# A five-stage pipelined decoder kernel on one core: stage results written where the next stage reads them, small operations moved between VectorE, GpSimd and ScalarE, and new orders for four engines

## The chip, the core and the metric

The kernel runs on one core of a Trainium2 chip. The metric is the device time in microseconds (us), median of several runs of the same program. Engines are named as in the profile: PE is TensorE's matmul, PEld its weight load, DVE is VectorE, ACT is ScalarE, POOL is GpSimd, SP is SyncE, which issues the DMAs. A line name such as L662 is a line of the kernel before.

## What is computed

32 samples of 128 tokens by 128 features go through a decoder block: self-attention with 16 heads whose queries, keys and values are the input itself, a post-norm, cross-attention to a context inside a band of 64 tokens, a post-norm, and two layers of a local transformer (8 heads of 64, rotary position coding, l2-normalised queries and keys, a gated MLP with gelu), with a last post-norm. Cut to what matters here:

```python
x = _layernorm(x + _L0_attn_ref(x, weight))                 # stage "self"
x = _layernorm(x + _L0_xattn_ref(x, ctx, ctx, Wq, ..., bo)) # stage "cross"
# two layers, stages "local0" and "local1":
h = shift_token(x); q, k, v = split(h @ wqkv)
q = q / clip(norm(q), 1e-12) * qs;  k = k / clip(norm(k), 1e-12) * ksc
q, k = rotary_xpos(q, k)
x = x + softmax(masked(8 q k^T)) v @ wo
h = shift_token(x); h = (h - mean) / sqrt(var + 1e-05) * lg + lb
a, g = split(h @ w1 + b1);  x = x + (a * gelu(g)) @ w2 + b2
# after both layers:
x = _layernorm(x + local(x))
```

`_layernorm` is `(x - mean) / sqrt(var + 1e-05)`.

## The kernel before

**Pipeline.** One sample is one tile of 128 by 128. The program runs 37 iterations n = 0 to 36. In iteration n the stages work on different samples: self (letter S, and Z for its values) on sample n-1, cross (C) on n-2, local layer 0's attention (A is its head part, D its tail part) and the first half of its MLP (M) on n-3, the second half of that MLP (O) and layer 1's attention (B, E) on n-4, and layer 1's MLP (N, P) on n-5; `SKEW` holds these lags. Iterations 0 to 5 are written out (the fill), 6 to 31 are one body in a loop on every engine (26 passes), and 32 to 36 are written out again (the drain), with parts missing at both ends. Iteration 32 still has every part; 33 has no self stage, 34 no cross stage, 35 and 36 less still.

**What sets the order.** Each part is a Python generator per engine; a `yield` ends a step. `ORDER_TENSOR`, `ORDER_VECTOR`, `ORDER_SCALAR` and `ORDER_GPSIMD` are strings of letters: `weave` takes the next step of the part that each letter names. So these four strings alone fix the order in which an engine issues its work in an iteration. Every engine runs its own instructions strictly in that order and meets the others only at semaphores. Since an engine stops at the first wait that isn't met, all work that its string puts behind that wait stands too.

**The steps that the change touches.**

- Between stages the result is written to an `out` tile by DVE (`normalise`, L932; L1076 for local0), POOL copies it into the next stage's `x` (L1152, L1165, L1172), PE transposes that `x` (L621, L662), ACT copies the transpose to SBUF (`xT`, L823 and L824), and PE's projections follow (L665, L668, L672).
- The normalisations need 1/sqrt(variance + eps). DVE makes mean and variance (`bn_stats`, `bn_aggr`, L1052 or L928), POOL adds eps into a tile `ve` (L1119) and raises it to -0.5 (L1122, into `rs`), DVE applies it (L932, L1055). There are five of these per iteration.
- The l2 norms of local attention: ACT squares (L828), DVE sums (`ss`, L1016), POOL applies the floor 1e-24 (`sc`, L1188) and the power -0.5 (`rn`, L1191). There are four per iteration (keys and queries of two layers). POOL also adds the two rotary products (L1195 for keys, L1199 for queries), scales the keys (L1203) and, after the exponentials, multiplies `e` by the inverse sums (L1212).
- Self's scores are made twice: once in bf16 from `kb` and `qmb` for the row maximum (L518), then in f32 from `kT` and `qm` (L529) with the negated maximum added by a second product (L534). ACT's exponentials of the first pair of banks (L779) must be done before PE may fill the banks again with the second pair (the second L529, which waits for `exp_done`).
- ACT changes between gelu (L873) and exp (L779 or L848) twice per iteration. Each change needs an ACT_TABLE_LOAD, which the compiler puts directly ahead of the first activation of the other kind.

## Time and profile before

| | |
|---|---|
| time, median of 3 runs | 1459.94 us (1458.5 to 1462.15) |
| the profiled execution's own time | 1461.15 us |
| its span in the trace | 1459.3 us |
| steady pass of the loop (between two L572 of the trace, 1204.59 and 1246.59) | 42.00 us |
| iteration 32's L572 (the first after the loop) to the end | 170.8 us |
| TensorE clock over the span | 0.965 of full |

The page of the profile gives each engine's busy time as a share of the span, with the span in 40 slices beneath. The timeline gives instructions in order of time: start, duration, engine, line, operation, output and input tiles, shapes, and in brackets the idle time of that engine just before, with what ended it. A PE entry's duration runs past the start of the next one, because matmuls overlap at their ends; the distance between two starts is what a group takes of the engine.

### The profile page before, as it was taken

To read this page: it belongs to the slowest core of one execution; us is meant where nothing else is said; L and a number is where in the kernel's file an instruction comes from. 1 tells how busy PE (TensorE), PEld (TensorE's weight loads), DVE (VectorE), ACT (ScalarE), POOL (GpSimd) and SP (SyncE) were. 2 spreads that over 40 slices of the span, in tenths; PEclk is the share of its full clock that TensorE was granted. 3 is DMA by queue.
4 is the path that set the end of the run, shared out by engine and by line. 5 is a ranking of instruction groups with operands and counts; after the bars stand their busy time and mean duration, and the time that the engine had idled before them with its cause. 6 is when DMAs were issued, how large, how long until landed. Compare 5 with 4: busy or idle time off the path is not lost. (4 is left out here: it accounts for less than half of the span.)

```text
span 1459.3 us, 39524 instructions
## 1 busy us (share of the span) xinstructions
PE 1333.5 (91%) x12472; PEld 928.8 (64%) x12472; DVE 1026.3 (70%) x2900; ACT 938.5 (64%) x2563; POOL 885.3 (61%) x1291
## 2 busy tenths in 40 slices
PE   5889999999999999999999999999999999998864
PEld 3556666666666666666666666666666666666543
DVE  2467776777777777777777777777777777776431
ACT  1256765677776667777766677776666777765552
POOL 2046666666666666666667666666666666666542
PEclk8799999999999999999999999999999999998785
DMA  5000000000000000000000000000000000000000
GB/s 158 10 5 4 5 7 7 5 4 5 4 4 5 5 5 5 4 4 4 5 5 5 5 5 4 4 4 5 5 5 5 4 5 3 5 5 3 3 3 4
DMA packets 22220, 12.55 MB, mean 9 GB/s; under 512 B 5878, under 2 KB 21024, under 8 KB 22176
## 3 DMA queue, kind: packets, MB, share of 16 engines
q1 hardware_dynamic: 21600, 10.96, 2.6%
q10 hardware_dynamic: 576, 1.05, 0.2%
q8 instruction: 22, 0.36, 0.1%
q14 instruction: 22, 0.18, 0.0%
HBM read 9.91 MB, written 2.10 MB: 8 GB/s over the span
## 5 line engine op out<-in xcount | busy, mean ns | idle before, releaser
L1212 POOL TENSOR_TENSOR local_e<-local_e,local_rd 128x512 f32<-128x512 f32 x128 | 133.0, 1039 | 238.2 <-DVE local_rd L1033 238.2
L848 ACT ACTIVATE local_e<-local_ps,local_bias,local_rn 128x128 f32<-128x128 f32 x512 | 230.8, 482 | 7.3 <-DVE local_bias L1029 7.3
L1191 POOL TENSOR_TENSOR local_rn<-local_sc,half_neg 128x8 f32<-128x8 f32 x128 | 211.3, 1658 | 14.4
L586 PE MATMUL self_ps<-self_z,self_e 128*128 128x129 f32 x1024 | 155.8, 291 | 2.6 <-ACT self_e L779 1.4
L1024 DVE TENSOR_REDUCE local_m<-local_ps 128x4 f32<-128x512 f32 x128 | 87.8, 686 | 96.4 <-PE local_ps L509 96.4
L586 PEld LDWEIGHTS self_ps<-self_z,self_e 128*128 128x128 f32 x1024 | 130.7, 196 | 13.8 <-issue 2.7
L955 DVE SCALAR_TENSOR_TENSOR self_y<-self_ps,self_rd,self_y 128x128 f32<-128x128 f32 x448 | 133.3, 345 | 8.8 <-issue 0.6
L606 PE MATMUL local_ps<-wz,self_kT 128*128 128x512 f32 x256 | 134.1, 627 | 1.1 <-ACT local_v L832 0.6
L848 ACT ACTIVATION_READ_ACCUMULATOR local_e<-local_ps,local_bias,local_rn 128x1 f32 x512 | 117.4, 229 | 0.0
L828 ACT ACTIVATE local_sq<-local_ps 128x512 f32<-128x512 f32 x128 | 76.1, 595 | 61.4 <-PE local_ps L665 58.4
L665 PE MATMUL local_ps<-wqkv_s,local_xT 128*128 128x512 f32 x128 | 71.4, 639 | 26.6 <-ACT local_xT L824 26.6
L918 DVE TENSOR_REDUCE self_neg<-self_ps 128x4 bf16<-128x512 f32 x128 | 81.9, 681 | 16.6 <-DMA bo_r<-bo 10.0
L1007 DVE TENSOR_TENSOR local_cosp<-local_ps,cos_t 128x512 f32<-128x512 f32 x128 | 87.4, 683 | 6.5 <-ACT local_sq L828 6.2
L859 ACT ACTIVATE local_oT<-local_ps 128x512 f32<-128x512 f32 x64 | 40.1, 627 | 78.8 <-PE local_ps L709 78.8
L855 ACT ACTIVATE local_eT<-local_ps 128x512 f32<-128x512 f32 x128 | 70.9, 610 | 28.6 <-PE local_ps L703 28.5
L779 ACT ACTIVATE cross_e<-cross_ps 128x512 f32<-128x512 f32 x128 | 69.6, 601 | 27.4 <-PE cross_ps L499 27.4
L1011 DVE TENSOR_TENSOR local_sinp<-local_ps,sin_t 128x512 f32<-128x512 f32 x128 | 87.1, 681 | 0.0
L703 PE MATMUL local_ps<-con,local_e 128*128 128x128 f32 x512 | 76.2, 284 | 11.6 <-POOL local_e L1212 11.6
L1195 POOL TENSOR_TENSOR local_cosp<-local_cosp,local_sinp 128x512 f32<-128x512 f32 x64 | 81.1, 1267 | 5.7 <-DVE local_sinp L1011 5.7
L918 DVE TENSOR_REDUCE cross_neg<-cross_ps 128x4 bf16<-128x512 f32 x128 | 82.2, 683 | 3.3 <-PE cross_ps L499 3.0
L1016 DVE TENSOR_REDUCE local_ss<-local_sq 128x8 f32<-128x512 f32 x128 | 83.9, 676 | 0.0
L798 ACT ACTIVATE self_z<-local_ps 128x512 f32<-128x512 f32 x128 | 77.0, 603 | 9.5 <-PE local_ps L606 9.5
(172 smaller groups left out, 3392.6 us busy)
## 6 DMA issues: line engine op xcount, KB each, us to landing
self_xin<-x SPq DMA_DIRECT2D x32, 64.0 KB, 1.8
cross_cin<-ctx_in SPq DMA_DIRECT2D x32, 64.0 KB, 1.8
out<-local_out SPq DMA_DIRECT2D x32, 64.0 KB, 1.6
wqkv_s<-wqkv SPq DMA_DIRECT2D x2, 768.0 KB
wz<-w_heads ACTq DMA_DIRECT2D x4, 256.0 KB, 6.3
w_r<-w SPq DMA_DIRECT2D x2, 341.0 KB
con<-consts SPq DMA_DIRECT2D x1, 640.0 KB, 6.0
wo_s<-wo SPq DMA_DIRECT2D x2, 256.0 KB
```

Of the source, the lines that this page charges most:

```text
L586: last = nc.tensor.matmul(bank[:, 129 * j:129 * j + 129], s.e[:, h0 + j, :], s.z[:, h0 + j, :], start=True, stop=True)
L606: nc.tensor.matmul(LOC[l].b1 if g % 2 else LOC[l].b0, s.kT[:, :], wz[:, 512 * g:512 * g + 512], start=True, stop=True).then_inc(s.z_psum, 4)
L848: nc.scalar.activation(s.e[:, a, p, :], bank[:, 128 * p:128 * p + 128], ACT.Exp, bias=s.bias[:, a, p:p + 1], scale=s.rq[:, a, p:p + 1], ac ...
L918: nc.vector.tensor_reduce(s.neg[:, 32 * g:32 * g + GH], (s.odd if g % 2 else s.even).rearrange("p (j t) -> p j t", j=GH), AX.X, ALU.max, n ...
L955: nc.vector.scalar_tensor_tensor(out=s.y[:, h % 2, :], in0=bank[:, j, 0:128], scalar=s.rd[:, h:h + 1], in1=before, op0=ALU.mult, op1=ALU.a ...
L1007: nc.vector.tensor_tensor(s.cosp[:, a, :, :], heads, cos_t[l][:, a, :].unsqueeze(1).to_broadcast([128, LH, LD]), ALU.mult)\
L1011: nc.vector.tensor_tensor(s.sinp[:, a, :, :].rearrange("p h (u d) -> p h u d", u=2), halves[:, :, ::-1, :], sin_t[l][:, a, :].rearrange("p ...
L1016: nc.vector.tensor_reduce(s.ss[:, LH * a:LH * a + LH], s.sq[:, a, :, :], AX.X, ALU.add)\
L1024: nc.vector.tensor_reduce(s.m[:, a, :], bank.rearrange("p (c t) -> p c t", c=LH // 2), AX.X, ALU.max, negate=True)\
L1191: nc.gpsimd.tensor_tensor(s.rn[:, heads], s.sc[:, heads], half_neg[:, 0:LH], ALU.pow).then_inc(done, 8)
L1195: nc.gpsimd.tensor_tensor(s.cosp[:, 0, :, :], s.cosp[:, 0, :, :], s.sinp[:, 0, :, :], ALU.add).then_inc(s.k_roped, STEP)
L1212: nc.gpsimd.tensor_tensor(s.e[:, a, :, :], s.e[:, a, :, :], s.rd[:, a, :].unsqueeze(2).to_broadcast([128, LH // 2, 128]), ALU.mult)\
```

## The change

1. `normalise` writes self's result straight into cross's `x`, cross's result straight into local0's `x`, and L1076's sum straight into local1's `x`. The POOL copies into those tiles go, and so do the tiles `out` in between. PE's transposes now wait for DVE's signals (`cross_normed` and the like) instead of `x_copied`. Where the residual of the whole local block is needed later, POOL copies local0's `x` once into `keep`.
2. The addition of eps (`ve`) and the floor (`sc`) move from POOL to DVE, each right behind the instruction that makes its input, with a wait for it. POOL keeps the powers alone, now one step each.
3. Self's bf16 copies `kb` and `qmb` move from POOL to ACT.
4. Copying self's input into `self_x` stays on POOL. The table loads stay where they were, ahead of their first use.
5. All four order strings are new.

```diff
 ORDER_TENSOR = (
-    "OONAAONASPBPABPBCZSCBZSZZASACSBBDCSECSSCSDSDSDCSDEEMCCECME")
+    "ONOAAONABSPPBABPZSZBCSAAZCSDSCZSCBBSCSECSDDSSDCSDEEMCCECME")
...
-    "NANNSCBOBSSASAAAAABBBBBBAABDDEEPMMMSPSCC")
+    "NNSBASAAAABABBBBDDCEEMPMSCO")
...
                 nc.scalar.activation(s.kT[:, :], s.b0[:, 0:128], ACT.Copy).then_inc(s.xT_ready, STEP)
+                nc.scalar.activation(s.kb[:, :], s.b0[:, 0:128], ACT.Copy).then_inc(s.k_ready, STEP)
+                yield
+                act.wait_ge(s.q_wide, v + STEP)
+                nc.scalar.activation(s.qmb[:, :, :], s.qm[:, :, :], ACT.Copy).then_inc(s.low, STEP)
...
-                nc.vector.bn_aggr(s.mv[:, :], s.st[:, 0, :]).then_inc(s.moments, 8)
+                nc.vector.bn_aggr(s.mv[:, :], s.st[:, 0, :]).then_inc(s.moments, 4)
+                dve.wait_ge(s.moments, v + 12)
+                nc.vector.tensor_scalar(s.ve[:, :], s.mv[:, 1:2], EPS, None, ALU.add).then_inc(s.moments, 4)
...
                 if again(v):
-                    dve.wait_ge(LOC[0].x_copied, v)
-                normalise(s, v, s.out[:, :])
+                    dve.wait_ge(LOC[0].kept, v)
+                    dve.wait_ge(LOC[0].mid_done, v)
+                normalise(s, v, LOC[0].x[:, :])
...
                     nc.vector.tensor_reduce(s.ss[:, LH * a:LH * a + LH], s.sq[:, a, :, :], AX.X, ALU.add)\
-                        .then_inc(s.square_sum, 8)
+                        .then_inc(s.square_sum, 4)
+                    dve.wait_ge(s.square_sum, v + 8 * a + 4)
+                    nc.vector.tensor_scalar(s.sc[:, LH * a:LH * a + LH], s.ss[:, LH * a:LH * a + LH], 1e-24, None, ALU.max)\
+                        .then_inc(s.square_sum, 4)
...
-                    copy(s.x[:, 0, :], CROSS.out[:, :]).then_inc(s.x_copied, STEP)
+                        pool.wait_ge(LOC[1].base_bias, v)
+                    copy(s.keep[:, :], s.x[:, :]).then_inc(s.kept, STEP)
...
-                    nc.gpsimd.tensor_scalar(s.sc[:, heads], s.ss[:, heads], 1e-24, 1.0, ALU.max, ALU.mult).then_inc(done, 8)
-                    yield
-                    pool.wait_ge(done, v + 8)
-                    nc.gpsimd.tensor_tensor(s.rn[:, heads], s.sc[:, heads], half_neg[:, 0:LH], ALU.pow).then_inc(done, 8)
+                    nc.gpsimd.tensor_tensor(s.rn[:, heads], s.sc[:, heads], half_neg[:, 0:LH], ALU.pow).then_inc(done, STEP)
```

What the new strings do to the engines' order is shown at three places. The first is TensorE in the middle of the loop body, from the first pair of self's f32 scores (L529 with L534) to the second pair, which waits for the two exponentials of the first. Before:

```order
L529 MATMUL self_ps<-self_qm,self_kT 128x512 x2
L534 MATMUL self_ps<-self_negT,hot_b 128x128 x8
L678 MATMUL local_ps<-con,local_cosp 128x128 x4
L653 REGISTER_ALU
L685 MATMUL local_ps<-con,local_cosp 128x128 x4
L696 MATMUL local_ps<-local_kT,local_qT 128x128 x8
L509 MATMUL local_ps<-mask_n,ident_b 64x512 x4
L552 REGISTER_ALU
L518 MATMUL cross_ps<-cross_kb,cross_qmb 128x128 x8
L499 MATMUL cross_ps<-mask_w,ident_b 64x4x64 x4
L529 MATMUL self_ps<-self_qm,self_kT 128x512 x2
```

The same stretch of TensorE in the changed kernel:

```order
L529 MATMUL self_ps<-self_qm,self_kT 128x512 x2
L534 MATMUL self_ps<-self_negT,hot_b 128x128 x8
L518 MATMUL cross_ps<-cross_kb,cross_qmb 128x128 x8
L499 MATMUL cross_ps<-mask_w,ident_b 64x4x64 x4
L606 MATMUL local_ps<-wz,self_kT 128x512
L529 MATMUL self_ps<-self_qm,self_kT 128x512 x2
```

Between the two pairs the transposes L678 and L685, the local scores L696 and their mask L509 have gone elsewhere, and one value product L606 has come in.

The second place is ScalarE at the same point of the changed kernel's loop body, with the semaphore that an instruction waits for in brackets. Lines are those of the changed kernel (its L852 was L848, its L802 was L798).

```order
L815 ACTIVATE cross_kT<-cross_ps,bk_c 128x128
L779 ACT_TABLE_LOAD [waits self_scores_t_psum]
L779 ACTIVATE self_e<-self_ps 128x512
L779 ACTIVATE self_e<-self_ps 128x512 [waits self_scores_t_psum]
L852 ACTIVATE local_e,local_den<-local_ps,local_bias,local_rn 128x128 [waits local0_bias_ready]
```

As before, the table load carries the wait for the scores; the two exponentials now follow each other directly, where before a copy of local1's `qT` stood between them.

The third place is GpSimd, where it handles the rotary sums and the norms of the two layers. Before, from the start of layer 1's part:

```order
L1195 TENSOR_TENSOR local_cosp<-local_cosp,local_sinp 128x512
L1188 TENSOR_SCALAR local_sc<-local_ss 128x8
L1191 TENSOR_TENSOR local_rn<-local_sc,half_neg 128x8
L1199 TENSOR_TENSOR local_cosp<-local_cosp,local_sinp 128x512
L1203 TENSOR_TENSOR local_cosp<-local_cosp,local_rn 128x512
L1188 TENSOR_SCALAR local_sc<-local_ss 128x8 x2
L1191 TENSOR_TENSOR local_rn<-local_sc,half_neg 128x8 x2
```

And in the changed kernel (L1183, L1187, L1179 and L1191 are there what L1195, L1199, L1191 and L1203 were):

```order
L1183 TENSOR_TENSOR local_cosp<-local_cosp,local_sinp 128x512
L1179 TENSOR_TENSOR local_rn<-local_sc,half_neg 128x8 x2
L1187 TENSOR_TENSOR local_cosp<-local_cosp,local_sinp 128x512
L1191 TENSOR_TENSOR local_cosp<-local_cosp,local_rn 128x512
L1179 TENSOR_TENSOR local_rn<-local_sc,half_neg 128x8
```

The floors have left GpSimd, and the first of the two powers in a row is now that of layer 0's queries; before, it stood behind all of layer 1's rotary work.

## Rows read from the trace of the kernel before

**Rows 1.** The page, part 1: busy time, share of the span, instructions.

```profile
PE 1333.5 (91%) x12472; PEld 928.8 (64%) x12472; DVE 1026.3 (70%) x2900; ACT 938.5 (64%) x2563; POOL 885.3 (61%) x1291
```

**Rows 2.** One pass: length, busy time of PE, PEld, DVE, ACT, POOL (count), clock.

```profile
1204.59:1246.59 42.00, 40.14 (x390) 28.18 (x389) 31.90 (x91) 29.13 (x80) 27.57 (x41) 1.00 0.02 5
```

**Rows 3.** Timeline of PE at the start of a pass.

```profile
737.95 0.33 PE L727 MATMUL cross_ps<-local_mid,con 128*128 128x64 f32 x2
738.90 0.30 PE L662 MATMUL local_ps<-con,local_x 128*128 128x128 f32 x1 [0.62 <-issue]
740.01 1.10 PE L665 MATMUL local_ps<-wqkv_s,local_xT 128*128 128x512 f32 x2 [0.81 <-ACT local_xT L824]
```

**Rows 4.** Timeline of DVE and POOL at the same place.

```profile
737.88 0.37 DVE L932 TENSOR_SCALAR cross_out<-cross_r,cross_mv,cross_rs 128x128 f32<-128x128 f32 x1 [0.69 <-POOL cross_rs L1122]
...
738.50 0.30 POOL L1096 TENSOR_SCALAR local_x<-cross_out 128x128 f32<-128x128 f32 x1 [0.35 <-DVE cross_out L932]
```

**Rows 5.** Timeline of PE, its other two idle gaps of a pass.

```profile
727.01 1.09 PE L709 MATMUL local_ps<-local_eT,local_v 128*64 128x128 f32 x16 [0.20 <-ACT local_eT L855]
...
735.64 1.16 PE L715 MATMUL local_ps<-wo_s,local_oT 128*128 128x128 f32 x8 [0.23 <-ACT local_oT L859]
```

**Rows 6.** Instruction groups of POOL and DVE: busy, mean ns | idle before.

```profile
L1191 POOL TENSOR_TENSOR local_rn<-local_sc,half_neg 128x8 f32<-128x8 f32 x128 | 211.3, 1658 | 14.4
L1199 POOL TENSOR_TENSOR local_cosp<-local_cosp,local_sinp 128x512 f32<-128x512 f32 x64 | 81.3, 1271 | 0.0
L1203 POOL TENSOR_TENSOR local_cosp<-local_cosp,local_rn 128x512 f32<-128x512 f32 x64 | 66.6, 1041 | 0.0
L1188 POOL TENSOR_SCALAR local_sc<-local_ss 128x8 f32<-128x8 f32 x128 | 32.0, 250 | 10.8 <-DVE local_ss L1016 0.2
L1096 POOL TENSOR_SCALAR self_qmb<-self_qm 128x512 bf16<-128x512 f32 x32 | 19.8, 617 | 0.3 <-POOL self_qm L1136 0.3
...
L1119 POOL TENSOR_SCALAR local_ve<-local_mv 128x1 f32<-128x1 f32 x96 | 18.3, 190 | 74.0 <-DVE local_mv L1052 63.7 <-DVE local_mv L928 7.7
```

**Rows 7.** Timeline of PE and ACT in the fill, no table load there.

```profile
18.47 0.39 PE L534 MATMUL self_ps<-self_negT,hot_b 32*128 32x128 bf16 x8
...
18.95 1.08 ACT L779 ACTIVATE self_e<-self_ps 128x512 f32<-128x512 f32 x2 [0.52 <-PE self_ps L534]
...
20.09 2.08 PE L529 MATMUL self_ps<-self_qm,self_kT 32*128 32x512 f32 x4 [1.23 <-ACT self_e L779]
```

**Rows 8.** Timeline of ACT in the drain: a table load behind a wait.

```profile
1390.62 1.28 ACT L848 ACT_TABLE_LOAD   x1 [1.87 <-DVE local_bias L1029]
```

**Rows 9.** Timeline of PE: what L606, L518 and L499 take.

```profile
708.66 1.02 PE L606 MATMUL local_ps<-wz,self_kT 128*128 128x512 f32 x2
709.62 0.40 PE L518 MATMUL self_ps<-self_kb,self_qmb 32*128 32x128 bf16 x8
...
717.18 0.40 PE L518 MATMUL cross_ps<-cross_kb,cross_qmb 32*128 32x128 bf16 x8
...
717.79 1.13 PE L529 MATMUL self_ps<-self_qm,self_kT 32*128 32x512 f32 x4
```

**Rows 10.** Timeline of POOL and DVE while POOL multiplies.

```profile
721.99 1.04 POOL L1212 TENSOR_TENSOR local_e<-local_e,local_rd 128x512 f32<-128x512 f32 x1 [3.12 <-DVE local_rd L1033]
...
722.66 0.39 DVE L1029 TENSOR_TENSOR local_bias<-local_m,local_rn 128x4 f32<-128x4 f32 x1
```

**Rows 11.** Timeline of POOL and DVE during a short POOL addition.

```profile
232.00 0.45 POOL L1223 TENSOR_TENSOR local_midb<-local_mid,local_base 128x128 f32<-128x128 f32 x1
232.13 0.41 DVE L932 TENSOR_SCALAR cross_out<-cross_r,cross_mv,cross_rs 128x128 f32<-128x128 f32 x1 [0.69 <-POOL cross_rs L1122]
```

**Rows 12.** Timeline of DVE at the end of a pass, first and last.

```profile
731.03 0.29 DVE L1039 TENSOR_TENSOR local_mid<-local_ps,local_x 128x128 f32<-128x128 f32 x1 [0.24 <-PE local_ps L715]
...
734.62 0.34 DVE L1057 TENSOR_SCALAR local_hn<-self_ps,local_mv,local_rs 128x64 f32<-128x64 f32 x1
```

**Rows 13.** Timeline of PE in iteration 34: the wait for weights.

```profile
1395.30 0.99 PE L703 MATMUL local_ps<-con,local_e 128*128 128x128 f32 x4 [4.38 <-POOL local_e L1212]
```

More of the change, by code:

```diff
@@ L1038, in attention_tail @@
                     dve.wait_ge(s.mid_bias, v)
-                nc.vector.tensor_tensor(s.mid[:, :], s.b1[:, 0:128], s.x[:, 0, :], ALU.add).then_inc(s.mid_done, STEP)
+                nc.vector.tensor_tensor(s.mid[:, :], s.b1[:, 0:128], s.x[:, :], ALU.add).then_inc(s.mid_done, STEP)
                 yield
@@ L1074, in mlp_tail @@
                     if again(v):
-                        dve.wait_ge(LOC[1].x_copied, v)
-                    nc.vector.tensor_tensor(s.out[:, 0, :], s.m0[:, 0:128], s.midb[:, :], ALU.add).then_inc(s.resid, STEP)
+                        dve.wait_ge(LOC[1].mid_done, v)
+                    nc.vector.tensor_tensor(LOC[1].x[:, :], s.m0[:, 0:128], s.midb[:, :], ALU.add).then_inc(s.resid, STEP)
                     yield
@@ L1083, in mlp_tail @@
                         dve.wait_ge(stored, v)
-                    normalise(s, v, s.out[:, 0, :])
+                    normalise(s, v, s.out[:, :])
                 yield
@@ L1114, in prepare_local, with inverse_root @@
                 pool.wait_ge(prep_v, PREP_V_LOCAL)
-            def inverse_root(s, v, moments_done, mv, out, done):
+            def inverse_root(s, v, moments_done, ve, out, done):
                 pool.wait_ge(moments_done, v + STEP)
-                nc.gpsimd.tensor_scalar(s.ve[:, :], mv[:, 1:2], EPS, 1.0, ALU.add, ALU.mult).then_inc(done, 8)
-                yield
-                pool.wait_ge(done, v + 8)
-                nc.gpsimd.tensor_tensor(out, s.ve[:, :], half_neg[:, 0:1], ALU.pow).then_inc(done, 8)
+                nc.gpsimd.tensor_tensor(out, ve[:, :], half_neg[:, 0:1], ALU.pow).then_inc(done, STEP)
             def self_stage(v):
@@ L1133, in self_stage @@
                 pool.wait_ge(s.xT_ready, v + STEP)
-                copy(s.kb[:, :], s.kT[:, :]).then_inc(s.k_ready, STEP)
-                yield
                 nc.gpsimd.tensor_tensor(s.qm[:, :, :], s.kT[:, :].unsqueeze(1).to_broadcast([128, GH, 128]), head_rows, ALU.mult)\
                     .then_inc(s.q_wide, STEP)
-                yield
-                pool.wait_ge(s.q_wide, v + STEP)
-                copy(s.qmb[:, :, :], s.qm[:, :, :]).then_inc(s.low, STEP)
                 if not again(v):
@@ L1151, in cross_stage @@
                     pool.wait_ge(s.resid, v)
-                copy(s.x[:, :], SELF.out[:, :]).then_inc(s.x_copied, STEP)
-                nc.gpsimd.tensor_tensor(s.xb[:, :], SELF.out[:, :], bo_r[:, :], ALU.add).then_inc(s.x_bias, STEP)
+                nc.gpsimd.tensor_tensor(s.xb[:, :], s.x[:, :], bo_r[:, :], ALU.add).then_inc(s.x_bias, STEP)
                 yield
-                yield from inverse_root(s, v, s.moments, s.mv, s.rs[:, :], s.rstd)
+                inverse_root(s, v, s.moments, s.ve, s.rs[:, :], s.rstd)
                 yield
```

53 lines of the change are left out of this document (20 added, 33 removed).

## The prediction

> **What bounds the kernel now.** I read the page first. TensorE is busy for 91% of the span, no other engine for more than 70% [rows 1]. I then cut one pass of the loop out of the windows view: 42.00 us, of which TensorE is busy 40.14 at full clock, while VectorE has 31.90, ScalarE 29.13 and GpSimd 27.57 [rows 2]. So TensorE's own work is the bound, and only 1.86 us per pass can be won by placing things better. TensorE's timeline shows where these lie, and there are four places. It waits 0.62 us before the transpose L662 and 0.81 us before L665 [rows 3], 0.20 before L709 and 0.23 before L715 [rows 5]. The first is a chain over three engines: VectorE writes cross's result (737.88 to 738.25), GpSimd copies it (738.50 to 738.80), and L662 starts at 738.90 [rows 3, 4]. The second is ScalarE's copy of the transpose, which the change leaves as it is.
>
> What matters is therefore not how busy VectorE or GpSimd get, but whether TensorE, which runs strictly in order, finds each input ready. I walked through the changed order with durations from the trace, one pass long.
>
> **Gains in a pass.** The GpSimd copy of 0.30 us and its two hand-overs go, and L662 can start when VectorE has written. GpSimd's eps addition (0.19 us [rows 6]) leaves the same chain and a VectorE one comes in, about even. VectorE had written by 738.25 and TensorE was free at 738.28 (738.90 less 0.62), so the whole 0.62 goes. L665 still follows L662 and a ScalarE copy directly: the 0.81 stays. The 0.20 before L709 goes if TensorE arrives later there than before, which the losses below see to. GpSimd loses about 3.9 us of its 27.6 per pass and ScalarE gains about 0.9 (0.62 for `qmb` [rows 6] and about 0.3 for `kb`); neither is on TensorE's path, since GpSimd mostly waits and ScalarE has 13 us idle.
>
> **Loss 1: the exponentials of self.** The changed TensorE order puts only L518, L499 and one L606 between the first pair of self's scores and the second. The second pair may not start before ScalarE has done two exponentials. In the fill, where no table load is needed, the L529 starts 1.23 us after L534 ended (two exponentials of 1.08 us together and the hand-overs) [rows 7]. In the loop the load of exp's table comes first. It is placed behind the wait for the scores: in the drain the same kind of load stood idle for 1.87 us until the value that its activation needed was there, and took 1.28 us [rows 8]. So the second pair can start 1.23 + 1.28 = 2.51 us after L534's end. In between TensorE has L518 and L499, 0.61 us from start to start (717.18 to 717.79), and L606 with 0.96 (708.66 to 709.62) [rows 9], and L518 begins 0.07 before L534 ends (0.39 of duration, 0.32 from start to start): 1.50 us of cover. That leaves TensorE idle for 1.01 us. Before, 3 us of work stood there and it cost nothing. The idle could be smaller only if the load came before the wait, and larger if L852's predecessor were late; I take 1.01, with 0.9 and 1.2 as bounds. Everything between L534 and this L529 that comes late is absorbed here.
>
> **Loss 2: VectorE's small operations behind GpSimd.** Four floors and five eps additions per pass come to VectorE. The trace has none there. The nearest rows are GpSimd's own 0.25 and 0.19 us [rows 6], and I take 0.25 for each with the wait for its predecessor. But some may cost more. A VectorE addition of 128x4 numbers that met a GpSimd multiplication ran 0.39 us and ended at 723.05, GpSimd's at 723.03 [rows 10]. A VectorE tensor_scalar of the kind that is now added, normally 0.37 [rows 4], ran 0.41 when GpSimd's addition lasted until 232.45, and ended 0.09 later [rows 11]. This is the pattern of an operation that is held until GpSimd lets go. The Trainium skill says so in SBUF — State Buffer, "SBUF: two separate sides": a VectorE operation in a two-port mode or with two SBUF inputs and a GpSimd operation exclude each other for a whole instruction. By that rule, the trace agrees, each added operation could wait out a full instruction of GpSimd.
>
> In the new orders layer 0's key floor falls due about 0.2 us after GpSimd begins `qm`, which takes as long as the key scaling (1.04 us [rows 6]); it would then hold VectorE for about 0.8 us. The floor for the queries comes late by the next rotary sum (1.27 us [rows 6]), by 0.1 to 0.3. Behind them on VectorE stand the gate product, for which L750 waits, and self's row maxima, for which L556 waits. With the distance that VectorE has there I get 0.3 at the first and 0.2 at the second: 0.5 us per pass. Bounds: 0 if the floors pass freely, and 1.3 if each is held for a whole rotary sum.
>
> **Loss 3: the end of the pass.** From layer 0's `mid` to its last normalised half VectorE takes 3.93 us (731.03 to 734.96) [rows 12]. Three eps additions join (0.75), and so does local1's normalisation (0.35, mostly overlapped: 0.25), while `self_r` may lose 0.2 that it spent beside a GpSimd addition. That is 0.8 later for L731 and, behind it, L715. L715 had waited for ScalarE until 735.64, 0.68 after VectorE was done [rows 5, 12], and 0.1 of this is L731 itself. So 0.6 is hidden and 0.2 is left, the old gap of 0.23 included. Bounds 0 and 0.8.
>
> **The pass:** -0.62 - 0.20 + 1.01 + 0.5 + 0.2 = +0.9 us, so 42.9. It applies to the 26 loop passes and to iterations 4, 5 and 32, which look the same: 29 x 0.9 = 26 us.
>
> **Fill and drain.** Here TensorE does wait for chains. The power for layer 0's queries used to stand behind layer 1's rotary work on GpSimd: a floor, a power, a rotary sum, a key scaling and two more floors, 0.25 + 1.66 + 1.27 + 1.04 + 0.5 = 4.7 us [rows 6]. It now stands ahead of these. Layer 0's exponentials need it, and TensorE then waited 4.38 us for their weights in iteration 34 [rows 13]. I put the gain at 4 us there, 4 in iteration 33 and 2 for 35 and 36 (shorter copies, an earlier L662): 10 us, bounds 4 and 14. In the first iterations shorter hand-overs and the earlier exponentials give 2 us, bounds -2 and 4.
>
> **Sum:** +26 - 10 - 2 = +14 us. The span is 1459.3, the profiled execution 1461.15 and the median of the runs 1459.94, so I add to the median: 1474 us, 1% slower.
>
> **Rivals.**
>
> - The small operations pass. The VectorE additions are not held, and the end of the pass has room: -0.62 - 0.20 + 1.01 = +0.2 per pass, 6 us in all, less 12 at the ends: 1454 us. For it: a 128x8 operation is short and most of GpSimd's time is one power, beside which I saw no hold. Chance 0.25. It spans 1448 to 1466.
> - Faster, one mechanism: the exponentials of self don't stop TensorE. If the table load ran ahead of the scores, 1.23 us would be needed against 1.50 of cover. With all of 0.62, 0.20 and 0.23 gone the pass is 40.95, 29 x 1.05 = 30 less, and 12 at the ends: 1418; with 0.5 of VectorE's delays, 1432. The point from which it decides is a load that begins before L534 ends. Against it: [rows 8]. Chance 0.12.
> - VectorE turns into the bound of stretches. By the skill's rule, if all four floors and the eps additions are held for whole GpSimd instructions (1.04 to 1.66 us) and the delays add up, the pass grows by 2 us: +58 - 12 = 1506 us. Against it: GpSimd's power did not hold VectorE, and VectorE has 10 us idle [rows 2]. Chance 0.12.
> - The change does nothing to the time: passes gain in one place what they lose in another, and the ends too, 1460 us. Chance 0.08.
> - The forecast, 1465 to 1486 us: 0.43.
>
> **How the numbers follow.** About 0.3% (4.4 us) is what a measurement of this kernel can tell from no change. Faster: the second rival (0.12) and 0.14 of the first, 0.26. Same: 0.09 of the first, 0.08 of the fourth and 0.03 of the forecast's low edge, 0.20. Slower: the rest, 0.54. The range 1446 to 1492 leaves out the faster rival but for 0.01 and the third but for 0.03; that is 0.2.
>
> **What the changed profile would show.** The idle before L662 gone, 0.81 before L665 unchanged; about 1 us idle before the second self L529, ended by ScalarE's `self_e`; the `sc` instructions of VectorE, some of 0.9 us instead of 0.15, ending with GpSimd's instruction; short gaps at the second L750 and at L556; L731 waiting for `local_hn`. A pass of 42.9 us, and a distance from iteration 32's L572 to the end of about 161 us. I am wrong if the L529 starts without a gap, if `sc` is always short, or if TensorE's clock falls below full in the loop.

## The result, and the profile after

The changed kernel takes 1483.26 us (median of 4 runs, 1481.8 to 1485.39), beside 1460.2 for the kernel before on the same chip. The ratio is 1.016, 95% interval 1.0139 to 1.0178: 1.6% slower, 9 us above the forecast of 1474 and inside its range. The profiled execution has a span of 1480.0 us; it is the fastest of the four and the one with the highest mean clock (0.963, the others 0.956 to 0.958). Line numbers are those of the changed kernel from here on, and those of its own file for each experiment (some lie a few lines off).

The page, part 1, the answer to [rows 1]:

```profile
PE 1331.0 (90%) x12472; PEld 927.5 (63%) x12472; DVE 1099.8 (74%) x3188; ACT 968.9 (65%) x2627; POOL 762.6 (52%) x843
```

TensorE does the same work in a longer span. VectorE has 288 instructions and 73.5 us more, GpSimd 448 instructions and 123 us less.

Two passes from the windows view (length, busy time of PE, PEld, DVE, ACT, POOL, granted clock), the answer to [rows 2]:

```profile
1183.70:1226.49 42.79, 39.90 (x391) 27.98 (x390) 34.05 (x101) 30.07 (x82) 23.74 (x26) 1.00 0.02 5
1226.49:1270.51 44.02, 41.32 (x391) 29.43 (x390) 34.17 (x101) 30.07 (x82) 23.73 (x26) 0.96 0.02 4
```

There are two kinds of pass. Most take 42.77 us, 0.77 more than before. Five of the 25 between iterations 7 and 32 take about 44.03, and only in these is the granted clock below 1.

The timeline of PE in the first of these passes, with every idle gap that the view marks (those over 0.15 us) and what stands before the long one; the answer to [rows 3, 5, 9]:

```profile
1188.07 0.93 PE L750 MATMUL cross_ps<-w_s,local_gate 114*128 114x128 f32 x6 [0.20 <-DVE local_gate L1079]
...
1198.09 0.22 PE L534 MATMUL self_ps<-self_negT,hot_b 32*128 32x128 bf16 x2
1198.11 0.22 PE L518 MATMUL cross_ps<-cross_kb,cross_qmb 32*128 32x128 bf16 x2
1198.26 0.30 PE L499 MATMUL cross_ps<-mask_w,ident_b 64*64 64x256 bf16 x4
1198.49 1.13 PE L606 MATMUL local_ps<-wz,self_kT 128*128 128x512 f32 x2
1200.81 1.13 PE L529 MATMUL self_ps<-self_qm,self_kT 32*128 32x512 f32 x4 [1.20 <-ACT self_e L779]
...
1203.64 0.91 PE L586 MATMUL self_ps<-self_z,self_e 128*128 128x129 f32 x6 [0.20 <-ACT self_e L779]
...
1219.97 0.30 PE L731 MATMUL self_ps<-con,local_hn 128*128 128x128 f32 x1 [0.34 <-DVE local_hn L1070]
...
1222.73 0.27 PE L662 MATMUL local_ps<-con,local_x 128*128 128x128 f32 x1
1223.81 1.10 PE L665 MATMUL local_ps<-wqkv_s,local_xT 128*128 128x512 f32 x2 [0.81 <-ACT local_xT L828]
```

L662 no longer waits, L709 and L715 neither, and the 0.81 before L665 is unchanged. New are 1.20 us before the second L529, 0.20 before L586, 0.20 before L750 and 0.34 before L731. L556 waits 0.14 here, just under what the view marks.

ScalarE at the long gap, the answer to [rows 8]:

```profile
1198.38 1.28 ACT L779 ACT_TABLE_LOAD   x1 [1.92 <-PE self_ps L534]
1199.68 1.09 ACT L779 ACTIVATE self_e<-self_ps 128x512 f32<-128x512 f32 x2
```

ScalarE stood idle for 1.92 us ahead of the load of exp's table, which began when L534's scores were there.

VectorE's first two floors of the pass, and GpSimd beside them:

```profile
1185.06 0.98 DVE L1027 TENSOR_SCALAR local_sc<-local_ss 128x8 f32<-128x8 f32 x1
1189.90 0.23 DVE L1027 TENSOR_SCALAR local_sc<-local_ss 128x8 f32<-128x8 f32 x1
```

```profile
1184.98 1.04 POOL L1144 TENSOR_TENSOR self_qm<-self_kT,con 128x512 f32<-128x512 f32 x1 [2.59 <-ACT self_kT L785]
1188.84 1.27 POOL L1187 TENSOR_TENSOR local_cosp<-local_cosp,local_sinp 128x512 f32<-128x512 f32 x1
```

Each floor began while GpSimd was at work and ended 0.02 us after GpSimd's instruction (1186.04 after 1186.02; 1190.13 after 1190.11). The other two floors of the pass take 0.17.

**Where the 20.7 us between the two profiled spans lie.** From the starts of L572: up to iteration 7 the changed kernel is 0.9 us ahead. The 25 passes from there to iteration 32 take 1075.48 us against 1049.94: 25 x 0.77 = 19.2, and 5 x 1.26 = 6.3 for the passes with a lower clock. From iteration 32 to the end it is 166.9 against 170.8, 4 us less. In that start each kernel has one pass at a granted clock of 0.96, the changed one from iteration 4 to 5 (43.48 us), the kernel before from 6 to 7 (44.16).

### The profile page after: what moved, and what is told of

The parts are those of the page before. It is cut to its first block and busy times, and to the rows that moved or that the text cites. A ratio compares the mean times of both kernels' runs of the same rounds, so it can differ in the third digit from the quotient of the medians.

```text
span 1480.0 us, 39442 instructions
## 1 busy us (share of the span) xinstructions
PE 1331.0 (90%) x12472; PEld 927.5 (63%) x12472; DVE 1099.8 (74%) x3188; ACT 968.9 (65%) x2627; POOL 762.6 (52%) x843
## 5 line engine op out<-in xcount | busy, mean ns | idle before, releaser
L1179 POOL TENSOR_TENSOR local_rn<-local_sc,half_neg 128x8 f32<-128x8 f32 x128 | 210.1, 1648 | 208.3 <-DVE local_sc L1027 125.3
L852 ACT ACTIVATE local_e<-local_ps,local_bias,local_rn 128x128 f32<-128x128 f32 x512 | 236.7, 495 | 40.5 <-DVE local_bias L1040 40.5
L586 PE MATMUL self_ps<-self_z,self_e 128*128 128x129 f32 x1024 | 157.4, 297 | 8.4 <-ACT self_e L779 7.2
L586 PEld LDWEIGHTS self_ps<-self_z,self_e 128*128 128x128 f32 x1024 | 135.7, 200 | 23.7 <-issue 13.5
L606 PE MATMUL local_ps<-wz,self_kT 128*128 128x512 f32 x256 | 144.7, 648 | 1.8 <-ACT self_kT L785 1.0
L802 ACT ACTIVATE self_z<-local_ps 128x512 f32<-128x512 f32 x128 | 76.9, 601 | 91.6 <-PE local_ps L606 91.6
L852 ACT ACTIVATION_READ_ACCUMULATOR local_e<-local_ps,local_bias,local_rn 128x1 f32 x512 | 124.1, 242 | 0.0
L529 PE MATMUL self_ps<-self_qm,self_kT 32*128 32x512 f32 x256 | 74.3, 657 | 36.2 <-ACT self_e L779 34.9
L1132 POOL TENSOR_TENSOR local_rs<-local_ve,half_neg 128x1 f32<-128x1 f32 x96 | 53.3, 556 | 82.3 <-DVE local_ve L1065 67.1
L665 PE MATMUL local_ps<-wqkv_s,local_xT 128*128 128x512 f32 x128 | 68.9, 620 | 26.6 <-ACT local_xT L828 26.6
L1183 POOL TENSOR_TENSOR local_cosp<-local_cosp,local_sinp 128x512 f32<-128x512 f32 x64 | 81.5, 1274 | 10.4 <-DVE local_sinp L1019 10.4
```

Source lines behind the costliest of these rows:

```text
L586: last = nc.tensor.matmul(bank[:, 129 * j:129 * j + 129], s.e[:, h0 + j, :], s.z[:, h0 + j, :], start=True, stop=True)
L606: nc.tensor.matmul(LOC[l].b1 if g % 2 else LOC[l].b0, s.kT[:, :], wz[:, 512 * g:512 * g + 512], start=True, stop=True).then_inc(s.z_psum, 4)
L852: nc.scalar.activation(s.e[:, a, p, :], bank[:, 128 * p:128 * p + 128], ACT.Exp, bias=s.bias[:, a, p:p + 1], scale=s.rq[:, a, p:p + 1], ac ...
L1179: nc.gpsimd.tensor_tensor(s.rn[:, heads], s.sc[:, heads], half_neg[:, 0:LH], ALU.pow).then_inc(done, STEP)
L1183: nc.gpsimd.tensor_tensor(s.cosp[:, 0, :, :], s.cosp[:, 0, :, :], s.sinp[:, 0, :, :], ALU.add).then_inc(s.k_roped, STEP)
```

## The experiments

Times are medians of 4 runs (e2 of 5). The ratio is to the kernel before, run beside each on the same chip, where it took 1462 to 1464 us (beside the changed kernel 1460.2, the first row), so ratios compare better than times from row to row. "Pass" is the distance of two L572 in the loop, from one profiled execution each.

| kernel | orders | on VectorE | exp table load | pass, us | time, us | ratio (95%) |
|---|---|---|---|---|---|---|
| before | old | - | | 42.00 | 1460.2 | 1 |
| e5 direct writes only | old | - | | 41.29 | 1438.47 | 0.984 (0.982-0.986) |
| e14 and kb, qmb on ScalarE | old | - | | 41.50 | 1445.39 | 0.988 (0.985-0.990) |
| e9 | old | floors | | 41.78 | 1450.72 | 0.991 (0.989-0.994) |
| e7 all code | old | floors, eps | | 42.71 | 1479.05 | 1.012 (1.010-1.013) |
| after | new | floors, eps | behind the wait | 42.77 | 1483.26 | 1.016 (1.014-1.018) |
| e2 | new | eps | behind the wait | 42.22 | 1473.97 | 1.009 (1.007-1.011) |
| e1 | new | floors, eps | early | 41.49 | 1436.56 | 0.982 (0.979-0.984) |
| e15 | new | 3 floors, eps | early | 42.00 | 1451.13 | 0.992 (0.988-0.995) |
| e6 | new | eps | early | 40.93 | 1420.65 | 0.972 (0.969-0.975) |
| e6b | new | - | early | 40.90 | 1420.02 | 0.972 (0.969-0.974) |
| e11 = e6, L662 earlier | new* | eps | early | 40.65 | 1412.17 | 0.965 (0.963-0.967) |
| e13 = after, more cover | new* | floors, eps | behind the wait | 43.32 | 1486.67 | 1.016 (1.014-1.018) |
| e8 = after, one load more | new | floors, eps | behind, and slower | 45.0 | 1569.95 | 1.074 (1.071-1.076) |

### The exponentials' gap: e1, e8, e13

The early load is one line more, behind the copy of cross's keys on ScalarE:

```diff
                 nc.scalar.activation(s.kT[:, :], s.b0[:, 0:128], ACT.Identity, bias=bk_c[:, :]).then_inc(s.k_ready, 8)
+                nc.scalar.activation(warm[:, :], SELF.z[:, 0, 128:129], ACT.Exp)
```

> The changed kernel with one more ScalarE instruction: an exponential of one column (128x1, its result is used by nobody) right behind the copy of cross's keys (L815), so that the exp table is loaded there and not behind the wait for self's scores (in the changed kernel the load at L779 stood idle for 1.92 us and then took 1.28). Theory A, the table load makes the gap: without it the second pair of self's scores needs 1.23 us after L534's end against 1.50 us of cover, so the 1.20 us of idle before the second L529 goes, and with it the 0.20 before L586; the five passes with a granted clock of 0.96 go too if the gap is what brings the clock down. Pass 41.4 us, 29 x 1.4 = 41 and 6 for the clock: 1483 - 47 = 1436 us. Rival B, the gap only hides another bound (VectorE's chain of the pass is late anyway): the idle time turns up at L556, L586 or L731, the pass falls by 0.4 at most, 1471 us.

It came out as theory A has it: 1436.56 us, pass 41.49. ScalarE in its timeline, and PE's second L529, which has no bracket and so no idle before it:

```profile
1074.38 1.28 ACT L816 ACT_TABLE_LOAD   x1
1075.67 0.20 ACT L816 ACTIVATE warm<-self_z 128x1 f32<-128x1 f32 x1
1076.30 1.08 ACT L779 ACTIVATE self_e<-self_ps 128x512 f32<-128x512 f32 x2 [0.42 <-PE self_ps L534]
```

```profile
1077.45 1.13 PE L529 MATMUL self_ps<-self_qm,self_kT 32*128 32x512 f32 x4
```

The load now lies in time in which ScalarE had nothing to do. The pass lost 1.28 us, just the load's length, and none of the 25 passes is below full clock in the profiled execution. The 0.2 before L586 stayed, which the expectation had wrong. The next run turns the screw the other way.

```diff
                 act.wait_ge(s.scores_t_psum, v + 4 * k + 4)
+                if s is SELF and k == 0 and again(v):
+                    nc.scalar.activation(warm2[:, :], SELF.z[:, 0, 128:129], ACT.Gelu)
```

> The opposite of the early load: the changed kernel with a second table load behind the wait for self's scores. ScalarE loads exp early (small exponential behind L815), then, behind the wait for L534's scores, runs a gelu of one column (its result is used by nobody), which needs a load of 1.28 us, and the exponentials need exp loaded again, 1.28. TensorE's idle before the second L529 becomes 1.20 + 1.28 + about 0.2. Theory A, this idle is what brings TensorE's clock down for some microseconds: more than 5 of the 25 passes show a granted clock below 1, and the gap's own cost is 1.5 us per pass: 1483 + 29 x 1.5 = 1527 us, and 1.25 for each further pass with a lower clock, up to 1550. Rival B, the lower clock has nothing to do with the idle: 5 passes again or fewer, 1527 us at most. Rival C, part of the longer gap is absorbed by work that waited later in the pass (L586, L731): 1515.

It took 1570 us, more than theory A's upper end. The gap did not grow as I had thought: ScalarE ran the gelu load ahead of the wait, but three loads of 1.28 then stood in a row and exp's ended at 681.73, so TensorE was idle for 2.32 us. PE at that gap, and two passes in the windows view:

```profile
682.88 1.23 PE L530 MATMUL self_ps<-self_qm,self_kT 32*128 32x512 f32 x4 [2.32 <-ACT self_e L782]
```

```profile
664.68:709.67 44.99, 41.17 (x392) 29.20 (x391) 34.07 (x101) 33.25 (x86) 23.72 (x26) 0.96 0.02 4
709.67:756.32 46.65, 42.86 (x392) 30.23 (x391) 34.16 (x101) 33.40 (x86) 23.73 (x26) 0.93 0.01 4
```

All 25 passes lie below full clock: 16 at 0.96 and 9 at 0.93. So the idle brings the clock down, and a longer one does it more often and for longer. Why a gap of 1.20 us does it in some passes and not in others stays open. In the changed kernel the place can be seen in small windows behind the gap, which ended at 1243.58:

```profile
1242.00:1244.00 2.00, 0.80 (x3) 0.30 (x4) 1.48 (x4) 1.99 (x6) 0.00 (x0) 1.00 0.00 0
1244.00:1246.00 2.00, 2.00 (x30) 1.34 (x27) 0.71 (x2) 2.00 (x8) 0.00 (x0) 0.90 0.00 0
1246.00:1248.00 2.00, 2.00 (x12) 1.80 (x10) 1.45 (x4) 2.00 (x7) 0.41 (x1) 0.50 0.00 0
1248.00:1250.00 2.00, 2.00 (x20) 1.88 (x20) 1.23 (x5) 1.65 (x9) 2.00 (x2) 0.74 0.00 0
```

TensorE has been back at work for 2 us when its clock falls to 0.50 (1.2 GHz instead of 2.4), and it is busy all through the last three windows. Their clocks of 0.90, 0.50 and 0.74 over 2 us each make 3.4 us at half clock in all.

The third run of this group leaves the load and adds cover, one L606 more between the two pairs (order strings of TensorE and ScalarE, one Z each moved):

```diff
-    "ONOAAONABSPPBABPZSZBCSAAZCSDSCZSCBBSCSECSDDSSDCSDEEMCCECME")
+    "ONOAAONABSPPBABPZSZBCSAACSDSCZZSCBBSCSECSDDSSDCSDEEMCCECME")
...
-    "OAANBSAPBASZZBBCAAZSCSSDZDSSBBDCDECEDDCEEDCCEEEM")
+    "OAANBSAPBASZZBBCAASCSSDZZDSSBBDCDECEDDCEEDCCEEEM")
```

> The changed kernel with the table load left where it is, behind the wait for self's scores, but with one more value product L606 (0.95 us) between the two pairs: the third Z of the TensorE order moves behind the L518/L499 group, beside the fourth, and on ScalarE its copy L802 moves behind the two exponentials. Theory A (the prediction's account, 2.51 us needed against the work in between): cover rises by 0.95, the idle before the second L529 falls from 1.20 to 0.25, the pass from 42.77 to 41.85, and no pass falls below full clock: 1483 - 29 x 0.95 - 6 = 1449 us. Rival B, the place that L606 leaves was itself cover (for cross's xT, or self_neg): idle of up to 0.9 turns up there, and the time stays above 1465.

Rival B: 1486.67 us, pass 43.32. PE in its pass:

```profile
1073.12 0.22 PE L556 MATMUL self_ps<-ident_b,self_neg 128*128 128x128 bf16 x1 [1.01 <-DVE self_neg L922]
...
1078.64 1.13 PE L529 MATMUL self_ps<-self_qm,self_kT 32*128 32x512 f32 x4 [0.42 <-ACT self_e L779]
```

The gap at L529 shrank, and the place that L606 left opened by 1.01 us: that product had covered VectorE's row maxima. In this pass no work is to spare as cover. The same run says something on the clock: with idle of 1.01 and 0.42 us in two places all 25 passes are at full clock. That is no safe limit: in the kernel before, the pass from iteration 6 to 7 is at 0.96, and its clock falls at 234.9, behind two gaps of 0.89 and 0.81 us:

```profile
233.20 0.30 PE L662 MATMUL local_ps<-con,local_x 128*128 128x128 f32 x1 [0.89 <-issue]
234.30 1.42 PE L665 MATMUL local_ps<-wqkv_s,local_xT 128*128 128x512 f32 x2 [0.81 <-ACT local_xT L824]
```

### The small operations on VectorE: e2, e6, e6b, e15

Floors back on GpSimd (e2: alone; e6: with the early load):

```diff
-                        .then_inc(s.square_sum, 4)
-                    dve.wait_ge(s.square_sum, v + 8 * a + 4)
-                    nc.vector.tensor_scalar(s.sc[:, LH * a:LH * a + LH], s.ss[:, LH * a:LH * a + LH], 1e-24, None, ALU.max)\
-                        .then_inc(s.square_sum, 4)
+                        .then_inc(s.square_sum, 8)
...
+                    nc.gpsimd.tensor_scalar(s.sc[:, heads], s.ss[:, heads], 1e-24, 1.0, ALU.max, ALU.mult).then_inc(done, 8)
+                    pool.wait_ge(done, v + 8)
```

> The changed kernel with the four floors per pass (sc) back on GpSimd, each directly ahead of its power, and all else as it is. Theory A, VectorE's floors are held while GpSimd works: the first floor of a pass took 0.98 us on VectorE and ended 0.02 us after GpSimd's qm, the third and fourth about 0.17. Without them VectorE is 1.4 us freer per pass, the 0.20 before L750 and the 0.15 that shows before L556 in some passes go: pass 42.5, 29 x 0.25 = 7 us less, 1476. Rival B, what is lost in a pass is the exponentials' gap alone, and GpSimd's extra 0.25 us in front of each power cancels it: 1483 +- 3.

> The changed kernel with both edits that helped alone: the small exponential behind L815, so that the exp table is loaded early (pass 41.49, 1436.6 us), and the four floors back on GpSimd (pass 42.22). Theory A, the two losses are separate places and add up: 0.55 us less per pass than with the early load alone, pass 40.94, 1436.6 - 28 x 0.55 = 1421 us, no pass below full clock. Rival B, with the gap gone VectorE and GpSimd are what TensorE waits for next: idle time turns up elsewhere and the pass stays above 41.3, 1432 us or more.

Both went with theory A, and e2's pass fell by more than its expectation has: 0.55 us. In e2 L750 starts 0.36 us earlier in the pass and L556 0.55, while the 1.20 before L529 is untouched; 4 of its 25 passes are at a clock of 0.96, and the profiled execution, 1466.7 us, is the fastest of the five, so its pass and its median don't belong to the same execution. On top of the early load the gain is again 0.56, so the two losses add up. e6 is the first kernel here that beats both e1 and e5: 1420.65 us.

In e6b the eps additions go back in the same manner, behind each `bn_aggr` and ahead of each power.

> The kernel with early load and floors back on GpSimd, and the five eps additions (ve) back on GpSimd too: what is left of the change is the direct writes, kb and qmb on ScalarE, and the new orders. Theory A (Loss 3 of the prediction), the eps additions make VectorE's chain at the end of the pass late: the 0.34 us before L731 goes, 40.6 us per pass, 9 us less than with the early load and the floors alone, 1412. Rival B, L731 waits because the new TensorE order asks for local_hn earlier and not because of eps: the gap stays within 0.1, and the time within 3 us.

The time is rival B's, within 1 us: the five eps additions on VectorE cost 0.03 us per pass here. Its reason is not, since the 0.34 before L731 does go, as theory A has it. Counted from L727 ahead of them, L731 starts 3.99 us later in e6 and 3.51 in e6b, but L739 behind L715 5.02 and 5.00: without the eps additions L715 waits 0.19 for ScalarE instead. They make L731 late, and the wait behind it hides that.

In e15 only the floor with `(l, a) == (0, 0)`, layer 0's keys, goes back:

```diff
+                        .then_inc(s.square_sum, 8 if (l, a) == (0, 0) else 4)
+                    if (l, a) != (0, 0):
```

> The kernel with the early load (41.49 a pass, 1436.6 us), with one of the four floors back on GpSimd: that of layer 0's keys, which took 0.98 us on VectorE while GpSimd ran self's qm. The other three, 0.17 to 0.23 us each, stay on VectorE. With all four back the pass was 40.93. Theory A, the loss is this one meeting: at least 0.36 of the 0.56 us comes back (the shift of L750), pass 41.0 to 41.15, 1425 us. Rival B, the loss is the time that four instructions with their waits take on VectorE, whichever: a quarter comes back, pass 41.35, 1433 us. Rival C, another small instruction is now held in its place: pass 41.5.

This is rival C and worse than it: 15 us slower than e1, from one floor that went from VectorE to GpSimd. The timelines of DVE and POOL show why:

```profile
1038.19 1.12 DVE L1029 TENSOR_SCALAR local_sc<-local_ss 128x8 f32<-128x8 f32 x1
```

```profile
1038.02 1.27 POOL L1193 TENSOR_TENSOR local_cosp<-local_cosp,local_sinp 128x512 f32<-128x512 f32 x1
```

```profile
1041.15 0.40 PE L518 MATMUL self_ps<-self_kb,self_qmb 32*128 32x128 bf16 x8 [0.54 <-DVE self_neg L923]
```

VectorE reached the second floor 0.17 us after GpSimd had begun a rotary sum and was held until it ended (1039.31, GpSimd 1039.29). Self's row maxima stood behind it, and L518 and L556 waited 0.54 and 0.43 us. In e1 the same floor came 1.07 us after that sum's start and took 0.22. Both engines moved: counted from L572, the floor came 0.36 us earlier (5.84 instead of 6.20), and the sum began 0.54 later (5.68 instead of 5.14), because the first floor now stood on GpSimd ahead of its power. So the cost of a floor is not its length but where in a GpSimd instruction it falls. SBUF — State Buffer, "SBUF: two separate sides", in the Trainium skill says of the pair of ports that VectorE and GpSimd share, for VectorE operations in a two-port mode or with two SBUF inputs: whoever comes first has it for its whole instruction. These rows agree.

### The same code in the old orders: e5, e14, e9, e7

e5 is the changed kernel's direct writes with everything else as before. e7 is the changed kernel with the old strings, cut where a step is gone:

```diff
 ORDER_GPSIMD = (
-    "NNSBASAAAABABBBBDDCEEMPMSCO")
+    "NNSCOBSAAAAABBBBABDDEEMMPSC")
```

e9 is e7 with the eps additions back on GpSimd, and e14 is e9 with the floors back too.

> The kernel before with part 1 of the change alone: stage results written straight into the next stage's input, GpSimd's copies gone, keep copied where kept stood; floors, eps, kb and qmb on GpSimd and all four order strings as before. Theory A, the 0.62 us before L662 was pure gain and stays won: pass 42.00 - 0.62 = 41.4, 29 x 0.62 = 18, 2 us more in the drain: 1440 us. Rival B, the time won turns up as a longer wait at L709 (0.20 before) and L715 (0.23), which are set by chains that don't start at L662: pass 41.8, 1454 us.

Theory A: 1438.47 us, pass 41.29. The idle before L662 is gone, which starts 0.10 us after VectorE's `local_x` ended (1096.55):

```profile
1096.65 0.30 PE L662 MATMUL local_ps<-con,local_x 128*128 128x128 f32 x1
1097.76 1.10 PE L665 MATMUL local_ps<-wqkv_s,local_xT 128*128 128x512 f32 x2 [0.81 <-ACT local_xT L824]
```

The first part of the change alone is worth 24 us (1462.05 beside it).

> Old orders, direct writes, floors and eps on GpSimd, and of the moved operations only kb and qmb on ScalarE (in the old orders the pass was 41.29 with direct writes alone, 41.78 with the floors on VectorE and kb, qmb on ScalarE). Theory A, the 0.49 us between these two is the floors': pass 41.3, 1438 us. Rival B, it is qmb's 0.62 on ScalarE ahead of the squares and value copies: pass 41.8, 1451 us.

In between: `kb` and `qmb` on ScalarE cost 0.21 us per pass, where I had costed them at nothing. `kb` stands ahead of `sq`, the gelu and `xT` on ScalarE; `sq` starts about 0.15 later in the pass than in e5, `xT` (L828) ends about 0.15 later, at 1191.51, and L665, which needs it, starts at 1191.65, later by as much. In e5 L665 followed L672 with no wait.

> All code of the changed kernel (direct writes, floors and eps on VectorE, kb and qmb on ScalarE) with the four order strings of the kernel before, cut by the steps that are gone and with one step more for qmb on ScalarE. In this TensorE order 3 us of work stand between the two pairs of self's scores, so the exponentials cost nothing. Theory A, the new TensorE order is what made the change slow: the pass is -0.62 for the copies, and +0.3 to +0.5 for the small operations on VectorE, 41.8, 1453 us, with no idle before the second L529 and no pass below full clock. Rival B, the small operations on VectorE are what made it slow: pass 42.6 or more, 1477 us.

Rival B, 1479.05 us: the new TensorE order is not what makes the moved operations dear. VectorE, GpSimd and PE in this kernel's pass:

```profile
1071.10 0.15 DVE L934 TENSOR_SCALAR local_ve<-local_mv 128x1 f32<-128x1 f32 x1
1071.23 0.90 DVE L1040 TENSOR_TENSOR local_bias<-local_m,local_rn 128x4 f32<-128x4 f32 x1
```

```profile
1071.07 1.04 POOL L1200 TENSOR_TENSOR local_e<-local_e,local_rd 128x512 f32<-128x512 f32 x1 [0.85 <-DVE local_rd L1044]
```

```profile
1072.96 0.94 PE L586 MATMUL self_ps<-self_z,self_e 128*128 128x129 f32 x6 [0.82 <-DVE self_y L961]
```

An old instruction, `local_bias` of 128x4 numbers, is held until GpSimd ends, because an eps addition ahead of it made it 0.2 us late. The eps addition itself was not held: it began 0.03 us after the same product of GpSimd and took its usual 0.15.

> The kernel with all code of the change but the old orders (pass 42.71, 1479 us), with the five eps additions back on GpSimd. There an eps addition of 0.15 us on VectorE stood ahead of layer 0's second local_bias (L1040, 128x4): with its wait it moved that instruction from 1070.98 to 1071.23, past the start of GpSimd's product L1200 at 1071.07, and it took 0.90 us instead of 0.16 and ended with GpSimd's; self_y behind it was late and TensorE idle for 0.82 before L586. Theory A, this meeting is the main loss of that kernel: without the eps addition L1040 is through before GpSimd starts, the 0.82 goes, pass 41.6 to 41.9, 1450 us. Rival B, the floors on VectorE or qmb on ScalarE make self_y late: L1040 is short or not, and the pass stays above 42.4, 1470 us or more.

Theory A, 1450.72 us. `local_bias` starts before GpSimd's product and slips through:

```profile
1052.90 0.16 DVE L1038 TENSOR_TENSOR local_bias<-local_m,local_rn 128x4 f32<-128x4 f32 x1
```

```profile
1053.04 1.04 POOL L1198 TENSOR_TENSOR local_e<-local_e,local_rd 128x512 f32<-128x512 f32 x1 [0.85 <-DVE local_rd L1042]
```

It had 0.14 us to spare. In the old orders the eps additions cost 0.93 us per pass and the floors 0.28; in the new ones 0.03 and 0.56. The same instructions, other meetings. (The two pairs were not taken in the same order: in the old orders the eps additions came on top of the floors, in the new ones the floors on top of the eps additions.)

### A further step: e11

```diff
-    "ONOAAONABSPPBABPZSZBCSAAZCSDSCZSCBBSCSECSDDSSDCSDEEMCCECME")
+    "ONAOAONABSPPBABPZSZBCSAAZCSDSCZSCBBSCSECSDDSSDCSDEEMCCECME")
```

> The kernel with early load and floors on GpSimd (40.93 a pass, 1420.65 us), with the start of the TensorE order changed so that L662 of layer 0 stands ahead of the second group of MLP products (L744) and not behind it. L665 then has 0.75 us of work between it and L662, and waits only for ScalarE, which is at gelu (L877) until 0.2 us after L662's usual start and then copies for 0.58. Theory A: of the 0.81 before L665 about 0.5 goes, 0.2 comes back before L662, which now waits for VectorE's local_x: pass 40.65, 1413 us. Rival B, the second half of the MLP products is late by what L662 waits, and with it the gate product L750: pass 40.9, within 3 us of 1420. Rival C, worse, since L662 waits for the whole chain of cross's normalisation: 1430.

Theory A in the time: 1412.17 us, pass 40.65, 3.5% faster than the kernel before. The 0.81 before L665 is 0.24; half of what that frees is given back elsewhere in the pass, about 0.14 in waits too short for the view to mark and 0.14 in TensorE's busy time.

## Why the prediction was right, and where it wasn't

Between the profiled spans the change cost 20.7 us where 14 were forecast. The pass was nearly right, 0.77 instead of 0.9, which is 3 us less over 25 passes. The clock, which had no term, added 6. From iteration 32 on 4 us were won where 9 were forecast (10, less the 0.9 of iteration 32's pass). Up to iteration 7 the changed kernel was 0.9 us ahead where it should have been 0.7 behind; the first iterations were not taken apart. That the total came out so near is in part luck, for the terms of the pass are off by more than their sum. The runs give them as a chain from the kernel before to the changed one, one edit at a time except in the third row, which has two:

| edit | pass, us | difference | the prediction's term |
|---|---|---|---|
| before to e5: direct writes | 42.00 to 41.29 | -0.71 | -0.62 |
| e5 to e14: kb, qmb on ScalarE | to 41.50 | +0.21 | 0 |
| e14 to e6b: new orders, load early | to 40.90 | -0.60 | -0.20 |
| e6b to e6: eps on VectorE | to 40.93 | +0.03 | +0.2 (Loss 3, 0.23 of old gap included) |
| e6 to e1: floors on VectorE | to 41.49 | +0.56 | +0.5 (Loss 2) |
| e1 to after: load behind the wait | to 42.77 | +1.28 | +1.01 (Loss 1) |
| sum | | +0.77 | +0.9 |

The third row holds what the prediction had at nothing: the new order saves TensorE work. Where L518 follows L534 directly, the two groups run in turns and take 0.34 us together (1197.92 to 1198.26 in the changed kernel). In the old orders they stood apart, here in e14, with 0.32 from L534 to the next start and 0.33 from L518:

```profile
1202.91 0.39 PE L534 MATMUL self_ps<-self_negT,hot_b 32*128 32x128 bf16 x8
1203.23 0.66 PE L678 MATMUL local_ps<-con,local_cosp 128*128 128x128 f32 x4
...
1205.68 0.40 PE L518 MATMUL cross_ps<-cross_kb,cross_qmb 32*128 32x128 bf16 x8
1206.01 0.30 PE L499 MATMUL cross_ps<-mask_w,ident_b 64*64 64x256 bf16 x4
```

That is 0.31 us at each of two places in a pass, about 0.6, against the 0.20 that the prediction expected from L709. TensorE's busy time in a pass falls by less, from 40.12 us in e14 to 39.72 in e6b. No run changes this alone.

- **The gap before L662** went as forecast, and 0.09 more with shorter waits earlier in the pass.
- **The exponentials' gap** was the right mechanism with the right need: L534's last product ended at 1198.31, L529 started at 1200.81, 2.50 us where 2.51 was worked out [rows 7, 8]. Mis-sized was the cover, 1.50 us. L518 alternated with L534 instead of following it, so only 0.18 of L518 and L499 lay behind L534's end, where 0.54 was taken. L606 covers up to its own end, 1.12, where 0.96 was taken, the distance to a next start. Together 1.30, and the idle was 1.20.
- **VectorE held by GpSimd** was right in place (layer 0's key floor beside `qm`, the query floor by a rotary sum) and in size (0.36 at L750 and 0.19 at L556, where 0.3 and 0.2 stood). What I took from it was too simple: it is a cost of phase, and e15 shows that it can rise when a floor leaves VectorE. It is also not a cost of every small operation. The eps additions (128x1) take 0.153 to 0.157 us in all 160 cases each of the changed kernel and of e7, also beside GpSimd's product. So the first rival, that the small operations pass, was right for these five and wrong for the floors. The third, that all are held, did not come true: in the changed kernel one of four floors per pass lost more than 0.1 us.
- **The end of the pass** had the right mechanism and too large a size. The eps additions make L731 wait 0.34, and what ScalarE would have made L715 wait hides it: e6b against e6 leaves 0.03 of the forecast 0.2.
- **kb and qmb on ScalarE** were costed at nothing because ScalarE has 13 us idle per pass. That step was wrong: idle on average did not hide `kb` at the place where TensorE needs the `xT` that stands behind it, and it cost 0.21 (e14).
- **TensorE's clock** was the sign that I named for being wrong. It falls in 5 of 25 passes and costs 6.3 us. The prediction had no term for it, though it forecast the idle that brings it about; by its own sign it was wrong here.
- **The drain** gained 4 us, not 10. The wait of 4.38 us for the weights in iteration 34 [rows 13] did shrink:

```profile
1419.64 1.11 PE L703 MATMUL local_ps<-con,local_e 128*128 128x128 f32 x4 [1.07 <-POOL local_e L1200]
```

From L672 to L672 that iteration is 3 us shorter (36.3 instead of 39.3). But iteration 33, counted by the same L672, won 0.9 and not 4, since no such wait stood in it, and behind the last L672 nothing was won (38.7 us to the end in both). That step carried a wait of one iteration over to its neighbour without a row for it. The gain belongs to the new orders: from iteration 32 to the end the kernels with old orders take 170 to 172.6 us, those with new ones 164.3 to 166.9 (e8, with its long gaps, 168.6). That it is GpSimd's place for the layer 0 power, and no other letter, was not tried by itself.
- **Rival 2**, that the exponentials don't stop TensorE, named its condition: a load that begins before L534 ends. e1 makes it true and takes 1436.6, where the rival gave 1432 with VectorE's delays; e6 takes these away and takes 1420.7, where it gave 1418.

## What to carry to other kernels

An engine's table load that stands behind a wait belongs to the latency of the wait: where a compiler puts it at its first use, a small activation of the same table ahead of the wait moves it into idle time. Which side of the wait a load stands on is read from the trace, since e8's gelu load ran ahead of the same wait. Some small VectorE operations (128x8 floors, 128x4 additions) cost what is left of the GpSimd multiplication or sum that they meet, others (the 128x1 additions) don't, so a trace of before gives their place, not their price. Any edit on these two engines can change who meets whom: look for operations that end with GpSimd's. A meeting need not cost anything: in e6 a `local_bias` is held for 1.07 us (1183.82), twice as long as in e1, and the marked TensorE gaps of that pass are no longer than e1's. When several edits are made together, undo them one at a time in the profile: here one part was worth 24 us and was buried under two others.

## What the runs showed of the hardware that I had not expected

- An idle gap of 1.20 us brought TensorE's clock from 2.4 to 1.2 GHz for 3.4 us in 5 of 25 passes (after) and in 4 of 25 (e2), and one of 2.32 us did in 25 of 25 (e8), for 3.4 us in 16 of them and 6.8 in 9. Gaps of 1.01 and 0.42 us apart in a pass did in none (e13), but gaps of 0.89 and 0.81 close together did once in the kernel before. With the gap of 1.20 the clock fell 2.0 to 2.2 us after TensorE had begun to work again, with that of 2.32 between 0.15 before and 1.6 after.
- Products on different rows of the array alternate: L534 (rows 0 to 63 there) and L518 (64 to 127), eight each one after the other in the program, ran in turns (1198.09, 1198.11). So TensorE does not hold strictly to the order of its string here. Both together took 0.34 us from start to start (1197.92 to 1198.26), where L534 alone takes 0.31 (1170.54 to 1170.85).
- A VectorE operation of 128x8 numbers with one SBUF input is held by GpSimd as one of 128x4 with two is: 0.98, 1.12 and 0.90 us, each ending 0.02 us after GpSimd's instruction. An addition of 128x1 numbers is not held (0.15 in e7, begun 0.03 us after GpSimd's product). Beside GpSimd's power the 128x4 addition isn't either: in the kernel before it takes 0.16 us (1222.14, in powers that run from 1219.61 to 1222.87).
- A table load takes 1.28 us, and the next activation started 0.01 to 0.02 us after it in every row shown, where it had nothing else to wait for.
